# Small attentions: raw exponentials are transposed, reciprocal sums are applied after the attention, and VectorE's steps are cut finer

## The reference

```python
x = L0(x, ctx)    # one norm over (64, 256), 8 heads over 256 features as positions, + x
x = L1(x, ctx)    # layernorm of ctx, 16 heads of 16, + x            (stage b)
x = L2(ctx, x)    # keys and values from ctx and x, 16 heads, then rmsnorm and an MLP with gelu (stage e)
x = L3(x, ctx)    # self-attention (stage c), cross-attention and an MLP (stage f)

# each attention of L1, L2 and L3, for one head:
probs = softmax(q @ k.T * scale + mask)      # 64 x 64, or 64 x 128 in L2
out   = probs @ v
```

## Time and profile before

| what | value |
|---|---|
| median of 3 runs | 1367.39 us (1364.12 to 1369.77) |
| the profiled execution | 1367.11 us, span from first to last instruction 1365.4 us |
| PE busy | 1261.7 us, 92% of the span |
| DVE busy | 1066.3 us, 78% |
| ACT busy | 830.9 us, 61% |
| POOL busy | 680.1 us, 50% |

### The profile page before, as it was taken

How to read it: one execution, slowest core, us unless ns; L and a number is a source line. 1 busy time by engine, 2 the same in 40 slices (tenths; PEclk the granted TensorE clock), 3 DMA queues, 4 the chain that set the end, 5 groups by cost and what they waited for, 6 DMA issues and landing times. The chain is left out here.

```text
span 1365.4 us, 36895 instructions
## 1 busy us (share of the span) xinstructions
PE 1261.7 (92%) x13948; PEld 969.2 (71%) x13948; DVE 1066.3 (78%) x2386; ACT 830.9 (61%) x2117; POOL 680.1 (50%) x977
## 2 busy tenths in 40 slices
PE   7999999999999999999999999999999999979575
PEld 4766668676786877778677777767677776858454
DVE  4779787978879797886879788787878878786742
ACT  3667566655766766576665657667665766735332
POOL 3554454553655546364554636546463655554331
PEclk9999999999999999999999999999999999999786
DMA  8100000000000000000000000000000000000000
GB/s 319 26 14 18 2 18 6 22 6 7 17 12 17 7 23 6 7 17 6 22 7 22 6 7 17 12 17 6 23 6 7 17 9 4 1 7 2 5 5 4
DMA packets 23595, 25.90 MB, mean 19 GB/s; under 512 B 10624, under 2 KB 22912, under 8 KB 23168
## 3 DMA queue, kind: packets, MB, share of 16 engines
q1 hardware_dynamic: 23424, 23.55, 5.5%
HBM read 21.44 MB, written 2.10 MB: 17 GB/s over the span
## 5 line engine op out<-in xcount | busy, mean ns | idle before, releaser
L592 POOL TENSOR_SCALAR p_a<-p_a,rec_a 128x256 f32<-128x256 f32 x512 | 239.6, 485 | 163.6 <-DVE rec_a L547 163.4
L578 ACT ACTIVATE p_a<-bank,nmax_a 128x256 f32<-128x256 f32 x512 | 237.0, 475 | 98.7 <-DVE nmax_a L540 97.7
L540 DVE TENSOR_REDUCE nmax_a<-bank 128x2 f32<-128x512 f32 x256 | 166.4, 678 | 10.4 <-PE bank L490 9.8
L605 PE MATMUL bank<-ident,p_a 128*128 128x128 f32 x1024 | 148.4, 278 | 7.9 <-ACT p_a L578 3.2
L490 PE MATMUL bank<-k_a,q_a 64*128 64x256 f32 x1024 | 138.7, 396 | 4.3 <-ACT p_a L578 1.5
L605 PEld LDWEIGHTS bank<-ident,p_a 128*128 128x128 f32 x1024 | 113.2, 141 | 39.1 <-issue 30.0
L621 PE MATMUL attended<-p_a,v_a 128*64 128x256 f32 x1024 | 135.3, 390 | 4.3 <-DVE p_a L639 1.9
L490 PEld LDWEIGHTS bank<-k_a,q_a 64*128 64x128 f32 x1024 | 91.8, 186 | 31.5 <-issue 21.7
L578 ACT ACTIVATION_READ_ACCUMULATOR p_a<-bank,nmax_a 128x1 f32 x512 | 105.8, 207 | 0.0
L654 ACT ACTIVATE p_a<-bank 128x512 f32<-128x512 f32 x128 | 76.5, 600 | 44.3 <-PE bank L605 43.4
L819 POOL TENSOR_TENSOR e_p<-e_p,e_rec 128x1024 f32<-128x1024 f32 x32 | 60.8, 1901 | 84.7 <-DVE e_rec L765 84.6
(11 more groups left out here) (236 smaller groups left out, 3082.3 us busy)
## 6 DMA issues: line engine op xcount, KB each, us to landing
wb<-in_wb SPq DMA_DIRECT2D x1, 4096.0 KB, 12.3
wc<-in_wc SPq DMA_DIRECT2D x1, 4096.0 KB, 24.8
xc<-in_x SPq DMA_DIRECT2D x16, 128.0 KB, 2.6
xc<-in_ctx SPq DMA_DIRECT2D x16, 128.0 KB, 2.9
c_top<-in_ctx SPq DMA_DIRECT2D x16, 128.0 KB, 2.9
k_c<-in_ctx SPq DMA_DIRECT2D x16, 128.0 KB, 2.0
res_a<-in_x SPq DMA_DIRECT2D x16, 128.0 KB, 2.2
out<-y_out SPq DMA_DIRECT2D x16, 128.0 KB, 1.7
```

Of the source, the lines that this page charges most:

```text
L540: dve.tensor_reduce(nmax_a[:, n, e, :], ps[:, :].rearrange("p (q k) -> p q k", q=KT), AX.X, ALU.max, negate=True).then_inc(A.s["max"], 1)
L578: last = act.activation(p_a[:, j % 2, n, e, qt, :], ps[:, qt * D:(qt + 1) * D], ACT.Exp, bias=nmax_a[:, n, e, qt:qt + 1], accum_out=sum_a[ ...
L592: last = pool.tensor_scalar(p_a[:, j % 2, n, e, qt, :], p_a[:, j % 2, n, e, qt, :], rec_a[:, n, e, qt:qt + 1], 1.0, ALU.mult, ALU.mult)
L605: last = nc.tensor.transpose(ps[:, kt * D + qt * P:kt * D + (qt + 1) * P], p_a[:, j % 2, n, e, qt, kt * P:(kt + 1) * P], ident[:, :])
```

## The change

- The small attentions transpose the raw exponentials: PE's transposes wait for the sum (which is the last reader of `T.p`) and no longer for a multiplication on POOL, which is gone.
- POOL copies the 16 reciprocals of each row, each 16 times over, into a new tile `T.wide` (`pool_wide`, two copies of 128x128 for each attention). PE transposes these two tiles into the free half of bank "o", behind the attended values.
- ACT copies the attended values to `T.yT` as before. DVE then multiplies `T.yT` by the transposed reciprocals from the bank, in place, and frees the bank.
- `pe_values` is 2 products of 128 columns of weights and 256 columns of moving data; `act_values` is 4 instructions of 64 partitions x 128 elements.
- Waits that other waits already imply are left out, in all engines' programs.
- DVE's generators yield between dependent short instructions, so that the order can put others between them. `ORDER` and `BANK` are written anew for all engines.

```diff
 ORDER = {
     "sp": (
-        "nsksfkbndefkbfdebekdnbndbendekyfbdnekbyfdnekyfbndekyfbndekyfbndekbynfdekdbyfnekyfbdnekbfydnekyfbdnekbyfdnekyfy"
+        "nskskdefbnkdefbefbkdnbdnebdnkeyfbndekyfbdnekyfbdnekybfdnekyfbdnekyfbdnekyfbdnkebdyfnekyfbdnekyfbdnkeyfbdnekyfy"
...
-SOFTMAX = {"kblk": 1, "max": KT, "sub": KT, "exp": KT, "sum": KT, "rec": KT, "prob": KT}
+SOFTMAX = {"kblk": 1, "max": KT, "sub": KT, "exp": KT, "sum": KT, "rec": KT, "wide": KT, "att": 1}
...
+            T.wide = t("wide", [P, KT, P])
...
         def pe_values(T, i, name, w, srcT):
             ps = fill_bank(T, nc.tensor, i, name)
-            wv = w.rearrange("p k (g e d) -> p k g e d", e=2, d=HD)
-            for b in range(2):
-                for k in range(KT):
-                    for e in range(2):
-                        last = mm(ps[e * S:(e + 1) * S, b * P:(b + 1) * P], srcT[:, k, b * S:(b + 1) * S], wv[:, k, :, e, :],
-                                  start=k == 0, stop=k == KT - 1)
+            for k in range(KT):
+                last = mm(ps[:, 0:D], srcT[:, k, :], w[:, k, :], start=k == 0, stop=k == KT - 1)
             filled(T, last, i, name)
...
-                    pe.wait_ge(T.s["prob"], T.at(i, "prob", r + 1))
+                    pe.wait_ge(T.s["sum"], T.at(i, "sum", r + 1))
                     ps = fill_bank(T, pe, i, ("t", r, c))
...
+            pe.wait_ge(T.s["wide"], T.at(i, "wide", KT))
+            for f in range(KT):
+                last = pe.transpose(ps[:, D + f * P:D + (f + 1) * P], T.wide[:, f, :], ident[:, :])
             filled(T, last, i, "o")
...
                 dve.tensor_reduce(T.max[:, r, :], v.rearrange("p c h k -> p h c k"), AX.XY, ALU.max).then_inc(T.s["max"], 1)
+                yield
                 dve.wait_ge(T.s["max"], T.at(i, "max", r + 1))
...
+            yield
+            dve.wait_ge(T.s["att"], T.at(i, "att", 1))
+            ps = wait_fill(T, dve, i, "o")
+            ins = dve.tensor_tensor(T.yT[:, :, :], T.yT[:, :, :], ps[:, D:2 * D].rearrange("p (f q) -> p f q", q=P), ALU.mult)
+            release(T, ins, i, "o")
             yield
...
-            release(T, act.activation(T.yT[:, :, :], ps[:, 0:D].rearrange("p (f q) -> p f q", q=P), ACT.Copy), i, "o")
+            act.activation(T.yT[:, :, :], ps[:, 0:D].rearrange("p (f q) -> p f q", q=P), ACT.Copy).then_inc(T.s["att"], 1)
...
-            for r in range(KT):
-                yield
-                pool.wait_ge(T.s["rec"], T.at(i, "rec", r + 1))
-                v = heads_of(T, r)
-                pool.tensor_tensor(v, v, bc(bc(T.rec[:, r, :], 2, S), 1, blocks), ALU.mult).then_inc(T.s["prob"], 1)
...
+        def pool_wide(T, i):
+
+            pool = nc.gpsimd
+            for f in range(KT):
+                yield
+                pool.wait_ge(T.s["rec"], T.at(i, "rec", KT))
+                if i:
+                    written(T, pool, i - 1, "o")
+                heads = T.rec[:, :, :].rearrange("p r (g f e) -> p (r g) f e", g=QUADS // KT, f=KT)[:, :, f, :]
+                pool.tensor_copy(T.wide[:, f, :].rearrange("p (n e d) -> p n e d", n=QUADS, e=2), bc(heads, 3, HD)).then_inc(T.s["wide"], 1)
...
-            for e in range(2):
-                last = act.activation(T.v[e * S:(e + 1) * S, c, :, :, e, :],
-                                      ps[e * S:(e + 1) * S, 0:D].rearrange("p (b g d) -> p b g d", b=2, d=HD), ACT.Copy)
+            for b in range(2):
+                heads = ps[b * S:(b + 1) * S, 0:D].rearrange("p (g e d) -> p g e d", e=2, d=HD)
+                for e in range(2):
+                    last = act.activation(T.v[e * S:(e + 1) * S, c, b, :, e, :], heads[:, :, e, :], ACT.Copy)
             release(V, last, i, name)
...
             def score(u, j, n):
-                written(A, pe, i, ("qk", j, 0))
-                written(A, pe, i, ("qk", j, 1))
-                if i or j > 1:
-                    pe.wait_ge(A.s["att"], A.at(i, "att", 2 * (j - 1)))
+                if n == 0:
+                    if i or j > 1:
+                        pe.wait_ge(A.s["att"], A.at(i, "att", 2 * (j - 1)))
+                    written(A, pe, i, ("qk", j, 0))
+                    written(A, pe, i, ("qk", j, 1))
```

More of the change, by code:

```diff
@@ L542, in dve_a @@
                 yield
-                for e in range(2):
-                    written(A, dve, i, ("s", u, e))
                 if i or u > 1:
                     dve.wait_ge(A.s["prob"], A.at(i, "prob", 2 * (u - 1)))
+                written(A, dve, i, ("s", u, 1))
                 dve.reciprocal(rec_a[:, n, :, :], sum_a[:, n, :, :]).then_inc(A.s["rec"], 1)
@@ L610, in attend @@
                 h = 2 * j + e
-                for n in range(2):
-                    written(A, pe, i, ("x", 2 * j + n, e))
+                written(A, pe, i, ("x", 2 * j + 1, e))
                 if h == 0:
@@ L708, in pe_attention @@
                 written(V, pe, i, name)
-                for r in range(KT):
-                    written(T, pe, i, ("t", r, c))
+            written(T, pe, i, ("t", KT - 1, blocks - 1))
             ps = fill_bank(T, pe, i, "o")
@@ L752, in dve_attention @@
                 else:
-                    for c in range(blocks):
-                        for g in quads_of(r):
-                            written(T, dve, i, ("s", c, g))
+                    written(T, dve, i, ("s", blocks - 1, quads_of(r)[-1]))
                 v = heads_of(T, r)
                 dve.tensor_reduce(T.max[:, r, :], v.rearrange("p c h k -> p h c k"), AX.XY, ALU.max).then_inc(T.s["max"], 1)
+                yield
                 dve.wait_ge(T.s["max"], T.at(i, "max", r + 1))
@@ L798, in pool_spread @@
             else:
-                for g in range(QUADS):
-                    wait_fill(T, pool, i - 1, ("s", c, g))
+                wait_fill(T, pool, i - 1, ("s", c, QUADS - 1))
             written(V, pool, i, name)
@@ L805, in pool_attention @@
         def pool_attention(T, i, mask_add, mask_ready):
[L806 to L814 removed]
+            pool = nc.gpsimd
             for r in range(KT):
                 yield
[L817 to L819 removed]
+                mask_ready(pool)
+                written(T, pool, i, ("s", 0, quads_of(r)[-1]))
+                v = heads_of(T, r)[:, 0, :, :]
+                pool.tensor_tensor(v, v, bc(mask_add[:, :], 1, HB), ALU.add).then_inc(T.s["madd"], 1)
+        def pool_wide(T, i):
+            pool = nc.gpsimd
+            for f in range(KT):
+                yield
+                pool.wait_ge(T.s["rec"], T.at(i, "rec", KT))
[3 more added lines that the diff above has]
+                pool.tensor_copy(T.wide[:, f, :].rearrange("p (n e d) -> p n e d", n=QUADS, e=2), bc(heads, 3, HD)).then_inc(T.s["wide"], 1)
         def pool_residual(T, i, n, src, row, source, user):
@@ L1035, in act_b @@
             yield from act_attention(B, i)
-        def pool_b(i):
-            yield from pool_attention(B, i, None, None)
         def pe_e(i):
@@ L1091, in pool_e @@
             yield from pool_spread(E, i, 1, E, "k", "kblk_own")
-            yield from pool_attention(E, i, None, None)
+            yield from pool_wide(E, i)
             yield from pool_norm(E, i, 0)
@@ L1133, in pool_c @@
             yield from pool_attention(C, i, self_add, lambda pool: ready(pool, i))
+            yield from pool_wide(C, i)
         def pe_f(i):
@@ L1175, in pool_f @@
             yield from pool_attention(F, i, m4_add, lambda pool: pool.wait_ge(F.s["mask"], F.at(i, "mask", 2)))
+            yield from pool_wide(F, i)
             yield from pool_residual(F, i, 1, x5[:, :], 4, lambda pool: written(F, pool, i, "p"), "y")
```

154 lines of the change are left out of this document (79 added, 75 removed).

## The result

The changed kernel takes 1336.89 us (median of 4, 1336.17 to 1337.98), before took 1367.7 in the same runs: ratio 0.9777, 95% interval 0.9758 to 0.9796, 2.2% faster. The profiled execution took 1336.17 us with a span of 1334.1.

The account below looks back on a forecast made before the run. It took PE's own work in written order to bound 85% of the span, dependent steps the end: 1367.1 + 2.9 (PE) + 2 (DVE, ACT) - 10 (middle) - 3 (end) = 1359 us, range 1340 to 1381.

Parts of the forecast that it names:

- The finer steps on DVE: VectorE's cuts between dependent short instructions: they remove gaps of DVE's own, taken at 0 us, without bounds.
- rival B: PE's middle stays as open as before; only PE's work and the end count: 1367 us; chance 0.26.
- PE's work: TensorE's sum of added transposes, cheaper values and fewer mode changes: +2.9 us, between -4.3 and +19.8.
- The wide transposes: Two transposes of reciprocals on PE in each of 64 attentions, 0.11 us each: +14.1 us, upper bound 19.8.
- The values: PE's `pe_values` as two full products, 80 x 0.07 = 5.6 us less; bounds no gain and 12.8 us.
- changes of mode: PE's switches between full and partial array use fall from 835 to 773: 5.6 us less, bounds 0 and 5.6.
- POOL: 160 us of multiplications go, 128 copies at 0.3 us (38 us) come; busy time falls to some 550 us.
- DVE and ACT: Beside PE, 64 multiplications add 27 us on DVE, finer `act_values` 28 us on ACT; 4% let through: +2 us.
- The middle's waits: PE's open 45.7 us from 34 to 1200 us shrink: -10 us, bounds +20 and -23.
- The end: Last pair's chains shorten, `e` by 2.0 us, `f` and `c` by 0.5 each: -3 us, bounds 0 and -6.
- C: VectorE's multiplication comes too late for PE at the output projection: 14 us more, 1381 us; chance 0.16.
- D: POOL was holding back VectorE; its relief takes half of the middle's open 45.7 us: 1344 us; chance 0.15.

Follow-up runs that it names:

- new_coarse: The changed kernel with all 544 of VectorE's cuts put back together, each whole step standing where its first part stood: 1368.81 us.
- new_no_recip: The changed kernel without the two wide transposes and DVE's multiplication, so the division is missing from its output: 1316.83 us.
- old_mult_beside: The kernel before, transposes waiting for the sum, POOL doing the same multiplication on a tile nobody reads, division missing: 1361.98 us.
- old_no_mult: The kernel before with POOL's multiplication by the reciprocals left out, transposes waiting for the sum, division missing: 1352.02 us.
- new_pool_load: The changed kernel with POOL's 128 multiplications given back on a tile nobody reads, each behind a wide copy: 1384.66 us.
- new_softmax_late: The changed kernel with maximum and subtraction, sum and reciprocal put together, each whole step standing where its second half stood: 1385.51 us.
- old_fine: The kernel before with all 544 VectorE cuts, second halves by rule one step of another stage behind, in the old order: 1392.43 us.
- new_rule_softmax: The changed kernel with the softmax steps' second halves by rule one step of another stage behind the first: 1346.01 us.

## Why the prediction was wrong, by its own steps

**The step that failed** is a sentence in the part on DVE: "The finer steps on DVE remove gaps of its own; no row prices them, I take 0." It fell outside the bounds as well, since I gave it none. What the runs show in its place: with the cuts undone the time is 1368.8 us, 31 us more, of which some 9 are shown as the cuts' own. The trace of before could have given a bound: 604 of its DVE instructions follow their neighbour within 0.06 us and 1474 overlap it, 0.12 us between the two cases (below), for 544 cuts at most 65 us of DVE's stream (an estimate; the busy time shows 32). But the larger part of the mistake, as I read it, is that I treated the order as background, something in which arithmetic is exchanged. My sum of 1359 was one without the cuts; new_coarse, which is that kernel with the disturbance of its order in it, measures 1368.8, close to rival B's 1367.

**PE's work**, +2.9 forecast. The wide transposes: new_no_recip gives 18.0 us of PE's busy time and 21 us of time against the forecast 14.1; PE's share is inside my upper bound of 19.8. The values: 12 us of time and 15.9 of PE's busy time against the forecast 5.6 and a part of the 5.6 for changes of mode; the time is just inside the bound of 12.8. The count of changes of mode explains it: in PE's records the changed order with the old values has 900 of them, not 773, and 5.6 + 127 x 0.09 = 17 us. By PE's busy time the two parts are +2.1, near my +2.9; by the time they are +9, with the new multiplication's delay in it. The two new transposes take 0.27 us at the least and 0.37 in the median from their first start to that of the next piece, where I had 0.22.

**POOL**: copies at 0.29 to 0.34 us against the 0.3 taken, busy 568 against 550. No wait for the wide tiles over 0.2 us. Right.

**DVE and ACT**: the multiplication 0.41 us against 0.425; `act_values` four times 0.27 us, 86.9 us in all, within my bounds. ACT's 883.5 us against 860 are the table loads of the new order, which I had left out. DVE's busy time was to rise to 1090 and fell to 1041. With whole steps it is 1073.7 (new_coarse), so 32 us are the cuts. The other 19 us fit with POOL's multiplications being gone: DVE's instructions without the new ones last 21 us less in sum there than before.

**The middle's waits**, -10. The open time of the middle fell by 14.6 us. The size is near by luck as much as by reasoning, since that window also holds more of the program: old_mult_beside and old_no_mult show that the multiplication in the chain and on POOL was worth 16 us even in the old order, more than my 10 here and 3 at the end together, and new_coarse that the gain is not there without the cuts.

**The end**, -3. The two chains I worked out came as forecast: `e` 2.0 us shorter, `f` from its second sum (1311.88) to its projection (1316.47) 4.59 us against 5.19 before, 0.6 where I said 0.5. But from stage `e`'s projection of the last pair but one to the end it is 12.5 us less. PE's waits in that stretch show where, before (from 1221.4 us) and after (from 1200):

```profile
PE bank L659 <- DVE e_yT L849: 7.9, 2, 4.0
PE bank L704 <- POOL f_p L819: 7.4, 1, 7.4
PE bank L704 <- POOL e_p L819: 5.9, 1, 5.9
```
```profile
PE bank L712 <- DVE f_sum L772: 6.0, 1, 6.0
...
PE bank L671 <- DVE e_yT L870: 1.6, 1, 1.6
```

The waits for `e`'s and `f`'s multiplication became 7.3 us shorter, those for the normalised `e_yT` 6.3. The latter I had not in the end's sum. In the last pair's norm the slow L840 of the earlier trace rows (0.81 us) is 0.22 us now, because POOL's L803 (now L817) stands behind the norm's reciprocal root and no longer beside this step; that is the new order on POOL.

**The rivals.** B: the middle did not stay. C: absent in the changed kernel (L738 waits 2.5 us for `c_yT`, 0.9 for `f_yT` and 0.7 for `e_yT` in the whole run), but real: 24 us in the old order. I missed that the order had been made to avoid it. D's time of 1344 was the nearest. Its mechanism is there (21 to 27 us of DVE's instructions), but not as its sum had it: the middle stayed open for 31.1 us where D wanted under 25, and with whole steps, where DVE's old instructions are shorter by nearly as much (21 us against 27), nothing was gained. L849's 1.33 us, which I counted for it, end 0.15 us behind the POOL instruction beside them (L814, 1289.01 to 1290.27), not with it.

**What stays open.** The 31 us can't be shared out: undone one by one, values (12), POOL's relief (48), cuts (31) and order (49, with the cuts in it) give far more than the whole, because each loss contains the disturbance of an order that was written for all of them. What part of the 31 us of new_coarse is the place of the second halves and what is mere disturbance is not settled; between 9 us (covered gaps of the softmax steps alone) and 31 us is shown. Part of each loss is TensorE's clock: the mean granted clock is 0.980 in the changed kernel, 0.974 in new_pool_load and 0.969 in new_softmax_late, and PE is busy there for 1272.2 and 1276.5 us with the products that take 1257.8. How many us of each loss the clock makes was not measured.

## What to carry to other kernels

In a kernel whose instruction order is written out, ask of a change what orders it makes possible, not only what it costs in the present one: the same arithmetic gave +1.4% in the old order and -2.2% in its own. On the engine that others wait for, try cutting steps at their dependences, and place the halves by who waits for each: by rule in the old order the cuts saved busy time and lost 24 us (old_fine), by rule in the new order they kept all but 8 us of the gain (new_rule_softmax, softmax steps alone). Before trusting a loss that undoing a part brings, measure what a neutral disturbance of the same size costs.

## What the runs showed of the hardware that I had not expected

- On VectorE an instruction that reads its neighbour's result starts 0.034 us after that one's end, an independent one 0.082 us before it (medians over the changed kernel's records, sorted by the gap, not by dependence; the timelines shown have both kinds): 0.12 us for each dependent neighbour, almost as much as the shortest of these instructions last (0.14 to 0.22 us).
- POOL at 52 to 53% busy, where 43% was enough, made the kernel 3.6% slower (48 us), whether it multiplied or only filled a tile.
- While POOL did more, TENSOR_SCALAR instructions on VectorE lasted 9 us longer in sum whether POOL multiplied or filled; those with two inputs lasted 7 us longer beside multiplications and 2 beside fills.
- The instruction order alone changes how often ScalarE loads a table: 68 or 90 loads of 1.28 us for the same arithmetic.
